# Grouped table look-ups, row numbers copied ahead of their gathers, and 16-bit shift steps in a graph network on one core

## The reference

```python
edge_index = jnp.stack([src, dst])
h = jnp.maximum(_layernorm(x, axis=-1), 0.0)
x = x + _L0_gnn_ref(h, L0_gnn_W1, L0_gnn_b1, L0_gnn_W2, L0_gnn_b2, edge_index)      # two GCN layers
h = jnp.maximum(_layernorm(x, axis=-1), 0.0)
x = x + _L1_gnn_ref(h, edge_index, edge_type_34, ...)                               # relational layer, then a GCN layer
h = jnp.maximum(_layernorm(x, axis=-1), 0.0)
x = x + _L2_gnn_ref(h, edge_index, ...)                                             # two attention (GAT) layers
h = jnp.maximum(_layernorm(x, axis=-1), 0.0)
x = x + _L3_gnn_ref(h, edge_index, L3_gnn_W, L3_gnn_b)                              # one GCN layer
```

```python
seg = edge_type * n + dst
agg = jax.ops.segment_sum(x[src], seg, num_segments=N_REL * n)
cnt = jax.ops.segment_sum(ones, seg, num_segments=N_REL * n)
mean = agg.reshape(N_REL, n, -1) / jnp.maximum(cnt, 1.0).reshape(N_REL, n, 1)
h1 = jnp.einsum('rni,rio->no', mean, W_rel) + x @ W_root + b_rgcn
```

## Time and profile before

| | us |
|---|---|
| median of 3 runs (lowest, highest) | 2828.74 (2826.45, 2830.72) |
| the profiled execution, its own time | 2819.55 |
| its span from first to last instruction | 2817.9 |
| TensorE busy | 2367.2 (84%) |
| VectorE, ScalarE, GpSimd busy | 1543.5, 1074.6, 1046.5 |
| mean granted TensorE clock | 0.938 of full |

### The profile page before, as it was taken

The page is one execution under the profiler, slowest core; times in us unless marked ns, Lnnn a source line. Parts: engine busy times, 40 slices in busy tenths (PEclk is TensorE's granted clock), DMA queues, the critical chain, the costliest instruction groups (busy, mean ns, idle before and its releaser), DMA issues.

```text
span 2817.9 us, 50548 instructions
## 1 busy us (share of the span) xinstructions
PE 2367.2 (84%) x12981; PEld 2203.0 (78%) x13015; DVE 1543.5 (55%) x2626; ACT 1074.6 (38%) x1833; POOL 1046.5 (37%) x1442
## 2 busy tenths in 40 slices
PE   3677668869999999999999987687797879978799
PEld 1355668869998998998998985566697879978799
DVE  6655584464433433443443436677645786687634
ACT  3222312223433433433443435555423345446421
POOL 4766000115655655655555657766400000000000
PEclk9999878989999999999999996988899989989999
DMA  6000102454555554555455447766611110011102
GB/s 215 1 0 0 52 0 94 155 202 157 182 186 169 175 202 170 170 196 182 168 193 182 172 146 235 218 212 207 200 42 60 56 39 0 12 49 53 56 12 99
DMA packets 117614, 346.41 MB, mean 123 GB/s; under 512 B 28615, under 2 KB 29595, under 8 KB 117509
## 3 DMA queue, kind: packets, MB, share of 16 engines
q1 hardware_dynamic: 73045, 205.21, 20.3%
q0 software_dynamic: 44528, 140.69, 16.2%
HBM read 258.18 MB, written 91.47 MB: 124 GB/s over the span
## 4 chain that ended last, share of the span: by engine, by line
PE 30%; issue 19%; DMA 15%; POOL 13%; DVE 11%; POOLq 5%; ACT 4%; DVEq 2%; ACTq 0%; SPq 0%
PE ps L1496 14%; DMA stage<-inv_table,stage 12%; PE ps L1553 10%; POOL stage L683 5%; PE ps L1623 4%; POOL land L747 3%; POOLq L669 3%; POOL table L692 2%; DMA land<-messages,stage 2%; POOL stage L679 2%; PE ps L1487 1%; DVE h_act L1083 1%; POOL h_act L673 1%; ACT land L831 1%; DVE agg_w L1105 1%
## 5 line engine op out<-in xcount | busy, mean ns | idle before, releaser
L1496 PE MATMUL ps<-w_a,h_t 128*128 128x384 f32 x4968 | 913.1, 340 | 5.3 <-issue 3.1
L1496 PEld LDWEIGHTS ps<-w_a,h_t 128*128 128x128 f32 x4968 | 868.0, 190 | 12.0 <-issue 8.2
L1553 PE MATMUL ps<-xw,agg_w 128*128 128x384 f32 x2800 | 539.4, 355 | 119.0 <-DVE agg_w L1105 84.3
L1553 PEld LDWEIGHTS ps<-xw,agg_w 128*128 128x128 f32 x2800 | 524.6, 201 | 131.1 <-issue 114.5
L1496 PE MATMUL ps<-xw,h_t 128*128 128x384 f32 x2448 | 457.2, 344 | 0.0
L1401 DVE TENSOR_TENSOR h_t<-ps,h_t 128x256 fp32r<-128x256 f32 x408 | 172.7, 423 | 508.1 <-ACT h_t L939 508.1
L1496 PEld LDWEIGHTS ps<-xw,h_t 128*128 128x128 f32 x2448 | 434.6, 190 | 0.0
L939 ACT ACTIVATE h_t<-ps 128x256 fp32r<-128x256 f32 x408 | 157.0, 385 | 620.2 <-PE ps L1496 431.6
L1487 PE MATMUL ps<-ident,land 128*128 128x128 f32 x1176 | 169.9, 282 | 123.7 <-DVE land L1397 67.6
L1697 PE MATMUL ps<-xw,agg_w 128*128 x736 | 203.0, 419 | 75.2 <-DVE xw L1453 73.4
L1487 PEld LDWEIGHTS ps<-ident,land 128*128 128x128 f32 x1176 | 140.0, 144 | 148.9 <-issue 128.0
(11 more groups left out here) (225 smaller groups left out, 2237.3 us busy)
## 6 DMA issues: line engine op xcount, KB each, us to landing
land<-in_L_gnn_W_rel SPq DMA_DIRECT2D x68, 1152.0 KB, 7.6
messages<-land SPq DMA_DIRECT2D x136, 384.0 KB
land<-x_state SPq DMA_DIRECT2D x40, 384.0 KB, 3.1
messages<-land POOLq DMA_DIRECT2D x34, 384.0 KB, 2.6
land<-in_L_gnn_W SPq DMA_DIRECT2D x10, 1152.0 KB, 6.4
x_state<-land SPq DMA_DIRECT2D x30, 384.0 KB, 2.3
adj<-x_state SPq DMA_DIRECT2D x10, 384.0 KB, 3.1
h_act<-x_state SPq DMA_DIRECT2D x1, 3840.0 KB, 13.1
```

The lines of the kernel that those rows point to most:

```text
L1496: ins = pe.matmul(acc(h), h_t[:, a, k, :], w[:, b, k, h * HF:(h + 1) * HF], start=(k == 0 and a == 0 and b == 0), stop=(stop and k == KB - ...
L1553: ins = pe.matmul(ps[:, 2 + 2 * u + h, 0:wide], agg_w[:, a, b, :], xw[:, c, b, h * HF:h * HF + wide], start=first, stop=last, skip_group_c ...
```

## The change

It has three parts.

1. **Relation stage, GpSimd.** The keys of all 5 columns of a ring turn are copied at once (`take_keys`), at the end of the turn before. The 10 look-up transfers are issued over the first three of the four chunks (2, 2, 1 columns), each without a copy and a wait ahead of it; their results are awaited and copied back (`keep`) once, at the end of the turn. `gather` is split in `place` (the position and the node numbers), which goes to the front, and the transfer.
2. **Sum stage, GpSimd.** The row numbers of the next quad are copied (`take_rows`) between the second and the third gather of a quad, behind a wait until all 4 gathers of the quad before have landed (`Q.yready`). Each gather waits for its own buffer instead of the first one of a quad for four.
3. **First aggregation, VectorE.** Distances are unsigned 16-bit numbers instead of 32-bit ones; the zeroed tail of `shift_part` and its memset are gone, since the last instruction of a step adds only the part that is inside the row. `find_gaps` moves from the second tile to the first. The 11 steps are spread: two on the 2nd and 3rd tile, one on each later tile, the last one behind `place_chunks`. The addition of the node numbers moves behind the last step.

The diff, cut to its core:

```diff
-        shift_by = rank[:, 0:NP].bitcast(I32)
+        shift_by, shift_part = (rank[:, k * NP:k * NP + NP // 2].bitcast(U16) for k in (0, 1))
         absent, gaps, shift_bit = rank[:, NP:2 * NP], rank[:, 3 * NP:4 * NP], rank[:, 4 * NP:5 * NP]
-        shift_part = rank[:, NP:3 * NP - 128].bitcast(I32)
...
-            def gather(c, k, copies):
+            def place(c, k):
                 at = pool.value_load(chunk_pos[0:1, ds(c, 1)], min_val=0, max_val=NT * NR - 1)
                 pool.tensor_copy(stage[:, k:k + 1], node_list[:, ds(at, 1)]).then_inc(R.addr, 1)
-                pool.wait_ge(R.addr, copies)
-                pool.sem_inc(turn_taken, 1)
+            def gather(k):
                 pool.indirect_dma_start(out=x_ring[:, k, :], out_offset=None, in_=h_table,
                                         in_offset=bass.IndirectOffsetOnAxis(stage[:, k:k + 1], 0)).then_inc(R.got[k], 16)
-            def look_up(j, u):
-                at = RING + 4 * u
-                pool.tensor_copy(stage[:, at:at + 2], keys[:, :, ds(j, 1)].rearrange("p a n -> p (a n)")).then_inc(R.col_addr, 1)
-                pool.wait_ge(R.col_addr, j + 1)
-                pool.sem_inc(turn_taken, 1)
+            key_at = stage[:, RING:RING + 2 * PER].rearrange("p (a n) -> p a n", a=2)
+            found = stage[:, RING + 2 * PER:RING + 4 * PER].rearrange("p (a n) -> p a n", a=2)
+            def take_keys(j, n):
+                pool.tensor_copy(key_at[:, :, 0:n], keys[:, :, ds(j, n)]).then_inc(R.col_addr, 1)
+            def look_up(m):
                 for a, tab in enumerate((slot_table, inv_table.bitcast(I32))):
-                    pool.indirect_dma_start(out=stage[:, at + 2 + a:at + 3 + a], out_offset=None, in_=tab,
-                                            in_offset=bass.IndirectOffsetOnAxis(stage[:, at + a:at + a + 1], 0))\
-                        .then_inc(R.col_got[u], 16)
-            def keep(j, u, done):
-                at = RING + 4 * u + 2
-                pool.wait_ge(R.col_got[u], done)
-                pool.sem_inc(turn_taken, 1)
-                pool.tensor_copy(keys[:, :, ds(j, 1)].rearrange("p a n -> p (a n)"), stage[:, at:at + 2]).then_inc(R.col_kept, 1)
+                    pool.indirect_dma_start(out=found[:, a, m:m + 1], out_offset=None, in_=tab,
+                                            in_offset=bass.IndirectOffsetOnAxis(key_at[:, a, m:m + 1], 0))\
+                        .then_inc(R.col_got, 16)
+            def keep(j, n):
+                pool.tensor_copy(keys[:, :, ds(j, n)], found[:, :, 0:n]).then_inc(R.col_kept, 1)
+            take_keys(0, PER)
             for c in range(RING - 1):
-                gather(c, c, c + 1)
+                place(c, c)
+                pool.wait_ge(R.addr, c + 1)
+                gather(c)
             for c in range(RING - 2):
                 pool.wait_ge(R.got[c], 16)
                 pool.sem_inc(R.ready, 1)
@@ -701,30 +701,45 @@
                 for k in range(RING):
                     c = RING * i + k
                     ahead, near = (k + RING - 1) % RING, (k + RING - 2) % RING
-                    mine = (0, 1) if k == 0 else (k + 1,)
-                    for m in mine:
-                        look_up(PER * i + m, m % 2)
+                    place(c + (RING - 1), ahead)
+                    if k == 0:
+                        pool.wait_ge(R.col_addr, i + 1)
+                        pool.sem_inc(turn_taken, 1)
+                    for m in ((0, 1), (2, 3), (4,), ())[k]:
+                        look_up(m)
+                    pool.wait_ge(R.addr, c + RING)
+                    pool.sem_inc(turn_taken, 1)
                     pool.wait_ge(R.copied, c)
                     pool.sem_inc(turn_taken, 1)
-                    gather(c + (RING - 1), ahead, c + RING)
+                    gather(ahead)
                     pool.wait_ge(R.got[near], 16 * i + (16 if k < 2 else 32))
                     pool.sem_inc(R.ready, 1)
-                    for m in mine:
-                        keep(PER * i + m, m % 2, 32 * ((3, 2)[m % 2] * i + m // 2 + 1))
+                    if k == RING - 1:
+                        pool.wait_ge(R.col_got, 32 * PER * i + 32 * PER)
+                        pool.sem_inc(turn_taken, 1)
+                        keep(PER * i, PER)
...
+                        take_keys(PER * i + PER, PER)
...
             with pool.Fori(0, more) as v:
                 j = nc.s_assert_within(PER * fours + v, 0, COLS - 1, skip_runtime_bounds_check_because="the table has room for all")
-                look_up(j, 0)
-                keep(j, 0, 96 * fours + 32 * v + 32)
+                pool.wait_ge(R.col_addr, fours + v + 1)
+                pool.sem_inc(turn_taken, 1)
+                take_keys(j, 1)
+                pool.wait_ge(R.col_addr, fours + v + 2)
+                pool.sem_inc(turn_taken, 1)
+                look_up(0)
+                pool.wait_ge(R.col_got, 32 * PER * fours + 32 * v + 32)
+                pool.sem_inc(turn_taken, 1)
+                keep(j, 1)
+            kept = fours + more
...
+            def take_rows(quad, u):
+                j = pool.value_load(quad_col[0:1, ds(quad, 1)], min_val=0, max_val=ECP - QUAD)
+                pool.tensor_copy(stage[:, u * QUAD:(u + 1) * QUAD], edge_slot[:, ds(j, QUAD)]).then_inc(R.col_kept, 1)
+            take_rows(0, 0)
             with pool.Fori(0, pairs) as i:
                 for u in range(2):
-                    j = pool.value_load(quad_col[0:1, ds(2 * i + u, 1)], min_val=0, max_val=ECP - QUAD)
-                    pool.wait_ge(Q.ylow, i * LAND + (u + 1) * QUAD)
+                    pool.wait_ge(R.col_kept, kept + i * 2 + (u + 1))
                     pool.sem_inc(turn_taken, 1)
-                    pool.tensor_copy(stage[:, u * QUAD:(u + 1) * QUAD], edge_slot[:, ds(j, QUAD)]).then_inc(R.col_kept, 1)
-                    pool.wait_ge(R.col_kept, rest + i * 2 + (u + 1))
-                    pool.sem_inc(turn_taken, 1)
-                    for b in range(u * QUAD, (u + 1) * QUAD):
+                    for k in range(QUAD):
+                        b = u * QUAD + k
+                        if k == 2:
+                            pool.wait_ge(Q.yready, i * LAND + u * QUAD)
+                            take_rows(2 * i + u + 1, 1 - u)
+                        pool.wait_ge(Q.ylow, i * LAND + b + 1)
+                        pool.sem_inc(turn_taken, 1)
                         pool.indirect_dma_start(out=y_ring[:, b, :], out_offset=None, in_=messages,
...
-                link(dve.tensor_scalar(size, size, 2.0, None, ALU.max))
-                dve.memset(shift_part[:, NP:2 * NP - 128], 0).then_inc(K.dve, 1)
+                dve.tensor_scalar(size, size, 2.0, None, ALU.max).then_inc(K.dve, 1)
                 dve.wait_ge(K.dve, K.sizes)
             def shift_step(bit):
-                taken = shift_bit.bitcast(I32)
-                link(dve.tensor_scalar(taken, shift_by, 1 << bit, None, ALU.bitwise_and))
-                link(dve.scalar_tensor_tensor(shift_part[:, 0:NP], taken, 0.0, shift_by, ALU.is_gt, ALU.mult))
-                link(dve.tensor_tensor(shift_by, shift_by, shift_part[:, 0:NP], ALU.subtract))
-                at = 1 << bit
-                link(dve.tensor_tensor(shift_by, shift_by, shift_part[:, at:at + NP], ALU.add))
+                taken, at = shift_bit[:, 0:NP // 2].bitcast(U16), 1 << bit
+                link(dve.tensor_scalar(taken, shift_by, at, None, ALU.bitwise_and))
+                link(dve.scalar_tensor_tensor(shift_part, taken, 0.0, shift_by, ALU.is_gt, ALU.mult))
+                link(dve.tensor_tensor(shift_by, shift_by, shift_part, ALU.subtract))
+                link(dve.tensor_tensor(shift_by[:, 0:NP - at], shift_by[:, 0:NP - at], shift_part[:, at:NP], ALU.add))
...
-                dve.tensor_tensor(shift_bit, shift_by, iota_n[0:NR, :], ALU.add)
...
                 dve.wait_ge(K.pe, K.summed)
+                dve.tensor_tensor(shift_bit, shift_by, iota_n[0:NR, :], ALU.add)
...
-                bits = (NP - 1).bit_length()
+                assert (NP - 1).bit_length() == NT + 1
                 for t in range(NT):
                     if t < NT - 1:
                         counts_low(g, t + 1)
-                    if t == 1:
+                    if t == 0:
                         find_gaps()
-                    if 1 < t < NT - 2:
-                        for bit in (2 * t - 4, 2 * t - 3):
-                            if bit < bits:
-                                shift_step(bit)
+                    for bit in ((), (0, 1), (2, 3))[t] if t < 3 else (t + 1,):
+                        shift_step(bit)
                     if t == NT - 2:
```

17 lines of the change are left out of this document (8 added, 9 removed).

## The result

| | before | after |
|---|---|---|
| median (lowest, highest), us | 2827.99 (2826.45, 2830.72) | 2735.59 (2732.33, 2736.15) |
| the profiled execution, us | 2819.55 | 2736.14 |

The ratio is 0.967 with an interval of [0.9653, 0.9687]; predicted were 2742 us. In two later sets, on other chips than the first, the same changed relation stage lost more than it had gained; that is the main finding of the experiments. Which chip the result itself ran on is not on record.

A forecast was written before the change was run, and what follows sets the result against it. The prediction took GpSimd to pace the relation and sum stages and VectorE to be without a pause in the first aggregation. Terms -86 - 14 + 14 = -86 gave 2733.6 in the profiled execution's terms, a median of 2742 us, range 2700 to 2790.

The forecast's parts named there:

- Relation stage, -86: Relation stage: GpSimd's turn falls from 30.8 to 23.9 us, under TensorE's 27.9, so 950 us shrink to 864.
- not 4: Relation stage: GpSimd would have 4 us of slack a turn, 23.9 against TensorE's 27.9.
- the 2.6 us of waiting for a landing: Relation stage: each turn GpSimd still waits 2.6 us for the last gather but one, which lands 3.9 after issue.
- First aggregation, -14: First aggregation: 16-bit steps of 3.8 us instead of 5.4, spread over tiles, start the last finish at 434 instead of 448.16.
- steps no faster: Rival, first aggregation: 16-bit steps are no faster, 11 us less gain, 2753 us; chance 0.10.
- Sum stage, +14: Sum stage: longer quads of GpSimd cost +34 us, fewer waits for free buffers give back 20.
- The -20 for the buffers: Sum stage: 20 of 23.6 us of buffer waits go, through per-buffer waits and a slower GpSimd filling the ring less.
- +0.73 and +34: Sum stage: a quad of GpSimd grows by 0.73 us to 7.5, 46 times, +34 us in all.
- The load's 0.6: Sum stage: the value_load now stands open behind the landing wait and costs 0.6 us a quad.
- free wait: Rival, sum stage: the new landing wait costs nothing and per-buffer waits pay, -30 there, 2699 us; chance 0.18.
- TensorE's clock: Rival, relation stage: the clock falls when TensorE's pauses go, 238 us more if a quarter of chunks, 2980; chance 0.03.
- slower: Whole kernel: chance 0.03 of a time slower than before, from TensorE's clock falling when its pauses go.

The follow-up runs named there:

- rel_alone: The kernel before with only the relation stage's part of the change (grouped key copies, row numbers copied ahead): 2736.23 us against 2831.87, ratio 0.9663.
- steps_32bit: The whole change with the shift steps on 32-bit numbers, new order kept: 2968.53 us, 1.0451 of before; the unchanged whole change in that set took 2950.87.
- sum_alone: The kernel before with only the sum stage's part of the change (row copy behind a landing wait, per-buffer waits): 2850.58 us against 2831.87, ratio 1.0071.
- load_before_wait: The whole change with the load of the next quad's column ahead of the landing wait: 2917.00 us, 1.0291 of before; sum stage 329.8 against 355.8.
- free_per_quad: The whole change with one wait per quad for all four buffers instead of one per buffer: 2938.12 us, 1.0366 of before; sum stage 348.4 against 355.8.
- copy_at_3: The whole change with landing wait, column load and copy moved from ahead of a quad's third gather to ahead of its fourth: 2687.49 us, 0.9493 of before.
- after_again: The whole change, unchanged, run again in the third set on another chip: 2950.87 us against 2843.68 before, ratio 1.0375.

## Why the prediction was right, and where not

- **Relation stage, -86.** Right, in mechanism and size: 91.1 by the relation length, chunks 6.98 apart (6.99 taken), waits gone, clock 1.00. GpSimd's slack is 7.1 to 7.6 us a turn and not 4, above all because the 2.6 us of waiting for a landing came to (5.8 + 3.9 + 1.5 + 2.4)/34 = 0.4: GpSimd stands waiting for a buffer in the meantime. `rel_alone` shows that the part stands by itself. More than the 67.6 us of waits went because TensorE's busy time per matmul fell too, from 881.66/5193 = 169.8 ns to 844.64/5088 = 166.0, some 20 us in all; that its pipeline fills again after each wait would give this, but no run shows it apart.
- **First aggregation, -14.** Measured -15.9 by the last finish, -18.7 from the marks. The step came out at 11.65 - 7.90 = 3.75 (3.8 taken), the last finish at 432.3 (434 taken). Its rival, steps no faster, falls by `steps_32bit`. One reading under it was wrong: L1315 is the step's addition of 1280 32-bit numbers (`shift_by` is an `I32` view), which the profile lists as 2560 16-bit ones. Its 1483 ns are what the 32-bit subtraction beside it takes, so it did not show two elements in the time of one; the 0.8 taken from it was right by luck, as far as this row goes.

```profile
L1313 DVE TENSOR_TENSOR land<-land 34x1280 int32<-34x1280 int32 x11 | 16.3, 1483 | 0.4
```

  By *VectorE: DVE Perf Modes* of the Trainium skill (the perf-mode tier table) `tensor_tensor` on 16-bit data runs at twice the plain rate; the trace agrees (818 ns against 1483). For the three-operand form, which that table doesn't list, the trace alone speaks: 1483 against 1484.
- **Sum stage, +14.** Measured +18 (`sum_alone`) to +21.5. Both terms have the right sign; the quad was taken too short. The -20 for the buffers came: 23.6 us of waiting before, 2.7 after (see above). Without these waits a quad of GpSimd is (206.1 + 71.0 - 2.7 + 12.5 + 68.3)/46 = 7.72 after, and by the same sum of the earlier trace rows 6.79 before: +0.93 or +43 in all, not +0.73 and +34. With -21 that is +22. The quad shown, 7.46, is what was added up (7.5), also term by term: 5.32 from the fourth gather to the copy (5.2 taken), then 0.18, 0.68 and 1.28. The mean is longer: the wait ahead of the copy, with the load in it, is 66.9/43 = 1.56 where the quad shown has 1.25, and landings reach 6.7 us, where the sum took the median of 4.5 for all. The load's 0.6 is right (`load_before_wait`). Of the reasons given for the -20, `free_per_quad` speaks against the first, each gather waiting for its own buffer; the slower GpSimd is left. Rival "free wait" (-30) needed what the change did not do: moved one gather later (`copy_at_3`), the sum stage is 29 us shorter than before.
- **The total.** By these lengths the three parts add up to -91.1 - 15.9 + 21.5 = -85.5, and -86 was forecast. The agreement to half a microsecond is luck: the relation stage gave 5 us more than was taken, the first aggregation 2 more and the sum stage 7.5 less. The mechanisms and the signs of the three are not luck; the runs of the parts alone bear them out.
- **TensorE's clock.** That it would fall when TensorE's pauses go was wrong in the run of the result (1.00) and is the wrong way round in `after_again`: there it is 0.92, and in the turn shown it falls behind a new pause.
- **What the prediction missed.** It gave 0.03 to "slower", for a reason that did not occur. On one of the chips the change *is* slower, by 3.75%, in a way that none of its rivals names. The price of a stage was taken from one chip's trace, and the look-ups were costed as GpSimd's time alone.
